# A transformer layer on one core: the second feed-forward product split into rounded high and low parts

## The reference

```python
q, k, v = x @ w_q, x @ w_k, x @ w_v            # 16 heads of 64
p = softmax(causal_mask(q @ k.T / 8))          # per head, 1024 x 1024
x = layernorm(x + (p @ v) @ w_o)
h = x @ W_exp + b_exp                          # 128 -> 512
h = butterfly(h, up_weights)                   # 9 stages of 2x2 mixes over the 512 features
h = gelu(h + up_bias)                          # exact gelu
h = butterfly(h, down_weights)                 # 9 stages
y = h @ W_con + b_con                          # 512 -> 128
x = layernorm(x + y + down_bias)
```

## Time and profile before

| | |
|---|---|
| median of 3 runs | 1036.63 us (1035.93 to 1037.27) |
| profiled execution: span from the first to the last instruction | 1033.9 us, some 2.7 us under the median |
| instructions | 17745 |
| attention, up to the first up product of group 0 | 968.2 us |
| feed-forward part and end | 65.7 us |
| PE busy | 1007.6 us, 97% of the span |

### The profile page before, as it was taken

One profiled execution on the slowest core, in us unless ns is written; L12 is line 12 of the kernel. 1 busy time (PEld: TensorE's weight loads), 2 busy tenths in 40 slices (PEclk: granted clock), 3 DMA queues, 4 the chain that ended last, 5 costly groups with the idle time before them and its releaser, 6 DMA issues.

```text
span 1033.9 us, 17745 instructions
## 1 busy us (share of the span) xinstructions
PE 1007.6 (97%) x5816; PEld 697.8 (67%) x5816; DVE 772.2 (75%) x2093; ACT 612.4 (59%) x1245; POOL 760.4 (74%) x739
## 2 busy tenths in 40 slices
PE   6899999999999999999999999999999999999997
PEld 4566676676766676676666776667666766665697
DVE  8767777777777777877788787877778787875364
ACT  3556655666655656566655656666555656665543
POOL 7567887777768887777778887777778987777414
PEclk8799999999999999999999999999999999999999
DMA  6233222233222222232222222332223222320002
GB/s 190 62 85 81 51 65 54 60 83 84 63 63 62 66 68 55 63 83 63 77 69 62 63 53 55 81 83 63 76 50 80 62 57 53 83 64 22 22 11 73
DMA packets 48603, 68.72 MB, mean 66 GB/s; under 512 B 15191, under 2 KB 25083, under 8 KB 48510
## 3 DMA queue, kind: packets, MB, share of 16 engines
q1 hardware_dynamic: 48510, 67.57, 25.3%
HBM read 31.11 MB, written 2.36 MB: 32 GB/s over the span
## 4 chain that ended last, share of the span: by engine, by line
PE 88%; DMA 5%; DVE 3%; ACT 1%; issue 1%; POOL 1%; SPq 0%; ACTq 0%; POOLq 0%
PE O L722 25%; PE WORK L636 13%; PE SC L697 13%; PE SC L701 12%; PE WORK L649 6%; PE WORK L684 3%; PE WORK L612 3%; PE WORK L613 3%; PE WORK L614 3%; DMA R<-RROW 2%; PE WORK L777 2%; DMA RROW<-RCOL 1%; PE WORK L622 1%; PE WORK L624 1%; PE WORK L623 1%; DVE WORK L989 1%
## 5 line engine op out<-in xcount | busy, mean ns | idle before, releaser
L868 ACT ACTIVATE PR<-SC 128x512 f32<-128x512 f32 (+3 forms) x768 | 352.3, 490 | 263.7 <-PE SC L701 234.8
L517 POOL TENSOR_TENSOR SUM<-SUM,PR 128x1024 f32<-128x1024 f32 (+3 forms) x256 | 419.3, 1638 | 14.9 <-POOL SUM L526 0.5
L989 DVE CUSTOM_DVE_ANT_0 WORK<-WORK,CMASK 128x128 f32<-128x128 f32 (+3 forms) x512 | 239.3, 514 | 64.8 <-PE WORK L636 64.7
L697 PE MATMUL SC<-QH,KHL 128*128 128x512 f32 (+3 forms) x768 | 269.3, 356 | 3.1 <-ACT PR L868 3.1
L701 PE MATMUL SC<-QL,KH 128*128 128x512 f32 (+3 forms) x768 | 262.0, 347 | 2.8 <-DMA QL<-NROW 2.8
L502 POOL TENSOR_SCALAR_AFFINE_SELECT PR<-PR 128x256 f32<-128x256 f32 x256 | 106.0, 415 | 198.6 <-ACT PR L868 198.5
L636 PE MATMUL WORK<-KHL,QH 128*128 128x512 f32 (+3 forms) x768 | 226.2, 365 | 4.3 <-DMA KH<-KHL 3.3
L722 PE MATMUL O<-PR,VLO 128*64 128x512 f32 (+3 forms) x1024 | 199.9, 522 | 0.6 <-DVE OT L1073 0.2
L697 PEld LDWEIGHTS SC<-QH,KHL 128*128 128x128 f32 x768 | 145.5, 189 | 61.2 <-ACT PR L868 28.9
L636 PEld LDWEIGHTS WORK<-KHL,QH 128*128 128x128 f32 x768 | 136.7, 191 | 57.1 <-issue 34.5
L992 DVE TENSOR_REDUCE MP<-WORK 128x1 f32<-128x512 f32 x256 | 164.3, 684 | 4.7
(11 more groups left out here) (129 smaller groups left out, 1099.6 us busy)
## 6 DMA issues: line engine op xcount, KB each, us to landing
QH<-QH SPq DMA_DIRECT2D x128, 128.0 KB, 2.3
KH<-KHL SPq DMA_DIRECT2D x128, 128.0 KB, 2.3
R<-RROW SPq DMA_DIRECT2D x64, 256.0 KB, 3.9
SW<-in_L_ffn_up_weights_dram SPq DMA_DIRECT2D x9, 512.0 KB, 4.3
SW<-_L_ffn_down_weights_dram SPq DMA_DIRECT2D x9, 512.0 KB, 4.6
out_dram<-X SPq DMA_DIRECT2D x7, 256.0 KB, 2.3
X<-in_L_attn_x_BSE_dram SPq DMA_DIRECT2D x3, 512.0 KB, 4.2
X<-in_L_attn_x_BSE_dram SPq DMA_DIRECT2D x2, 256.0 KB, 3.0
```

The lines of the kernel that those rows point to most:

```text
L517: nc.gpsimd.tensor_tensor(total, total, prob(unit, s), ALU.add).then_inc(add_done, 1)
L697: nc.tensor.matmul(dst, KHL[:, par, h, kt * P:(kt + 1) * P], QH[:, par, h, q0:q0 + n], start=True, stop=False)
L868: nc.scalar.activation(prob(unit, s)[:, h, :], SC[use % NSC][:, 0:n], ACT.Exp, scale=K ** -0.5).then_inc(exp_done, 1)
L989: op = nc.vector.tensor_tensor_reduce(cols, cols, CMASK[:, CH - n:], 1.0, LOWEST, ALU.add, ALU.max, cell)
```

## The change

W2 is no longer copied to SBUF as fp32: ACT writes its high part to W2H and DVE its low part to W2L (in the space of XTH and XTL). The Gelu result of each group, 128 x 2048 values, is split the same way: ACT copies the high part (one instruction), and the low part is G - hi, by POOL alone for groups 0 to 2, and by DVE (first half of the columns) and POOL (second half) for groups 3 to 7. The parts lie in four pairs of slots in QH, QL, KHL and KH1, which the attention and the up products have finished reading (`SPLIT_PAIR`). The tables `SPLIT_AFTER` and `DVE_SPLIT_AFTER` say after which group's Gelus, and after which `residual` or `deviation`, a split stands in the list of its engine. `down(g)` then makes three fp32r products in place of one fp32 product: hi x W2H, hi x W2L, lo x W2H. It waits for the splits (`split_lo`, `split_lo_dve`); a Gelu waits for the split of the group whose place in G it takes, not for the down product.

```diff
--- before.py
+++ after.py
@@ -120,6 +120,11 @@
 FFN_PIECES = [(g * TPC, (g + 1) * TPC) for g in range(B * CHUNKS - 1)]
 FFN_PIECES += [(B * TILES - TPC, B * TILES - 2), (B * TILES - 2, B * TILES)]
 ACT_RESULTS = 3
+SPLIT_PAIR = [0, 1, 2, 0, 1, 2, 0, 3]
+POOL_SPLITS = 3
+SPLIT_ORDER = [0, 1, 2, 3, 4, 5, 7, 6]
+SPLIT_AFTER = {0: [0], 1: [1], 3: [2], 5: [3], 6: [4], 7: [5, 7, 6]}
+DVE_SPLIT_AFTER = {0: [3], 1: [4], 2: [5, 7], 3: [6]}
 X1_AT = {("x1", g): (UNITS - 1, g + 2 + 4 * (g > 2), 2) for g in range(EARLY_GROUPS)} | {("w2", 0): (UNITS - 1, 11, 2)}
 NORMALISE_AT = {t: ((t // TILES + 1) * PAIRS + 3 + t % TILES, 10) for t in range((B - 2) * TILES)}
 NORMALISE_AT |= {t: ((B - 1) * PAIRS + 3 + t % TILES // 2, 9 + t % 2) for t in range((B - 2) * TILES, (B - 1) * TILES)}
@@ -257,6 +262,11 @@
         up_b_row = w2t[0:1, :]
         x1_hi_slots = [T[:, 0, h, c * CH:(c + 1) * CH] for T in (QH, QL) for h in range(2) for c in range(CHUNKS)]
         x1_lo_slots = [T[:, 0, h, c * CH:(c + 1) * CH] for T in (KHL, KH1) for h in range(2) for c in range(CHUNKS)]
+        parity = lambda T, n: T[:, n, :, :].rearrange("p h s -> p (h s)")
+        split_pairs = [(parity(QH, 1), parity(QL, 1)), (parity(KHL, 1), parity(KH1, 1)),
+                       (parity(QH, 0), parity(KHL, 0)), (parity(QL, 0), parity(KH1, 0))]
+        W2H = XTH[:, 0:HID].rearrange("p (t d) -> p t d", t=HT)
+        W2L = XTL[:, 0:HID].rearrange("p (t d) -> p t d", t=HT)
         W1H = WST[:, :, :, :].rearrange("p a n c -> p (a n c)")
         W1L = WSV[:, :, :].rearrange("p a c -> p (a c)")
         wqkv_flat = WQKV[:, :, :].rearrange("p n c -> p (n c)")
@@ -298,6 +308,7 @@
         h1_added, stats_made = sem("h1_added"), sem("stats_made")
         x1_made, x1t_made, x1t_copied = sem("x1_made"), sem("x1t_made"), sem("x1t_copied")
         x1t_hi, w1_hi, w1_lo = sem("x1t_hi"), sem("w1_hi"), sem("w1_lo")
+        w2_hi, split_hi, split_lo, split_lo_dve = sem("w2_hi"), sem("split_hi"), sem("split_lo"), sem("split_lo_dve")
         hid_ready, gelu_done, y_ready, h2_made = sem("hid_ready"), sem("gelu_done"), sem("y_ready"), sem("h2_made")
         out_made, act_out_made, out_stored = sem("out_made"), sem("act_out_made"), sem("out_stored")
         shift_mult, shift_made = sem("shift_mult"), sem("shift_made")
@@ -350,6 +361,10 @@
             qc, kt = STEPS[s]
             n = CH - START[s] if n is None else n
             return PR[:, (unit * NS + s) % PRING, :, 0:n]
+
+        def hidden(g):
+
+            return G[g % (DOWN_LAG + 1)].rearrange("p t c -> p (t c)")
 
         block = ctx.enter_context(nc.Block())
 
@@ -563,8 +578,19 @@
                         compose(n)
                 add(u, NS - 1)
 
+            def split_low(k):
+
+                pool.wait_ge(split_hi, SPLIT_ORDER.index(k) + 1)
+                hi_part, lo_part = split_pairs[SPLIT_PAIR[k]]
+                cols = slice(0 if k < POOL_SPLITS else 2 * CH, HT * CH)
+                nc.gpsimd.tensor_tensor(lo_part[:, cols], hidden(k)[:, cols], hi_part[:, cols].bitcast(F32),
+                                        ALU.subtract).then_inc(split_lo, 1)
+
+            split_low(0)
+            split_low(1)
             pool.wait_ge(stats_made, B * TILES)
             deviation((B - 1) * TILES, B * TILES)
+            split_low(2)
             for n, (first, end) in enumerate(FFN_PIECES):
                 pool.wait_ge(x1_made, min(end, B * TILES))
                 pool.wait_ge(stats_made, B * TILES + end)
@@ -576,6 +602,8 @@
                     pool.wait_ge(shift_mult, n - ACT_RESULTS + 1)
                     nc.gpsimd.tensor_scalar(SHIFT[:, first:end], SHIFT[:, first:end], -1.0, None,
                                             ALU.mult).then_inc(shift_made, 1)
+                for k in DVE_SPLIT_AFTER.get(n, []):
+                    split_low(k)
 
 
         @block.tensor
@@ -766,16 +794,22 @@
                                      stop=True).then_inc(hid_ready, 1)
 
             def down(g):
-                pe.wait_ge(gelu_done, (g + 1) * HT)
+                pe.wait_ge(split_lo, SPLIT_ORDER.index(g) + 1)
+                if g >= POOL_SPLITS:
+                    pe.wait_ge(split_lo_dve, SPLIT_ORDER.index(g) + 1 - POOL_SPLITS)
                 if g < 2:
                     evacuated(LAST_OUT + g)
                     evacuated(NUMBER[UNITS - 1, ("w2", 0)])
                 else:
                     pe.wait_ge(h2_made, g - 1)
+                g_hi, g_lo = split_pairs[SPLIT_PAIR[g]]
                 for i in range(TPC):
+                    y = y_bank(g * TPC + i)[:, i * P:(i + 1) * P]
                     for t_ in range(HT):
-                        t = nc.tensor.matmul(y_bank(g * TPC + i)[:, i * P:(i + 1) * P], G[g % (DOWN_LAG + 1)][:, t_, i * P:(i + 1) * P],
-                                             W2[:, t_, :], start=t_ == 0, stop=t_ == HT - 1)
+                        cols = slice(t_ * CH + i * P, t_ * CH + (i + 1) * P)
+                        nc.tensor.matmul(y, g_hi[:, cols], W2H[:, t_, :], start=t_ == 0, stop=False)
+                        nc.tensor.matmul(y, g_hi[:, cols], W2L[:, t_, :], start=False, stop=False)
+                        t = nc.tensor.matmul(y, g_lo[:, cols], W2H[:, t_, :], start=False, stop=t_ == HT - 1)
                     if any(end == g * TPC + i + 1 for _, end in FFN_PIECES):
                         t.then_inc(y_ready, 1)
 
@@ -826,9 +860,12 @@
             def evacuate(u, f, at):
 
                 w, free = WORK[at % NWORK], work_free[at % NWORK]
-                if f[0] in ("max", "out", "w2", "wo", "con", "bias"):
+                if f[0] in ("max", "out", "wo", "con", "bias"):
                     return
                 act.wait_ge(work_ready, at + 1)
+                if f[0] == "w2":
+                    hi(W2H, w[:, :].rearrange("p (t d) -> p t d", t=HT)).then_inc(w2_hi, 1)
+                    return
                 if f[0] == "x1":
                     hi(x1_hi_slots[f[1]], w[:, :]).then_inc(x1t_hi, 1)
                     return
@@ -901,13 +938,20 @@
                 for t_ in range(HT):
                     act.wait_ge(hid_ready, g * HT + t_ + 1)
                     if t_ == 0 and g > DOWN_LAG:
-                        act.wait_ge(y_ready, g - DOWN_LAG)
+                        act.wait_ge(split_lo, g - DOWN_LAG)
+                        if g - DOWN_LAG > POOL_SPLITS:
+                            act.wait_ge(split_lo_dve, g - DOWN_LAG - POOL_SPLITS)
                     nc.scalar.activation(G[g % (DOWN_LAG + 1)][:, t_, :], hid_banks[t_], ACT.Gelu,
                                          bias=BIAS1[:, t_:t_ + 1]).then_inc(gelu_done, 1)
                 n = g - (EARLY_GROUPS - 2)
                 if 0 <= n < B * CHUNKS - EARLY_GROUPS:
                     act.wait_ge(x1t_made, n + 1)
                     hi(x1_hi_slots[EARLY_GROUPS + n], O[(EARLY_GROUPS + n) % 2][:, :]).then_inc(x1t_hi, 1)
+                for k in SPLIT_AFTER.get(g, []):
+                    if k in (3, 4, 5, 6):
+                        act.wait_ge(y_ready, k - 3 + 1)
+                    act.wait_ge(gelu_done, (k + 1) * HT)
+                    hi(split_pairs[SPLIT_PAIR[k]][0], hidden(k)).then_inc(split_hi, 1)
             for n in range(ACT_RESULTS, len(FFN_PIECES)):
                 act.wait_ge(shift_made, n - ACT_RESULTS + 1)
                 for t in range(*FFN_PIECES[n]):
@@ -1042,8 +1086,8 @@
                     nc.vector.tensor_copy(BIAS1[:, :], w[:, 0:HT]).then_inc(free, 1)
                     dve.wait_ge(bc_made, 1)
                 elif f[0] == "w2":
-                    dve.wait_ge(work_ready, at + 1)
-                    nc.vector.tensor_copy(w2t, w[:, :]).then_inc(free, 1)
+                    dve.wait_ge(w2_hi, 1)
+                    lo(W2L, w[:, :].rearrange("p (t d) -> p t d", t=HT), W2H).then_inc(free, 1)
 
             def add_bc(g):
 
@@ -1143,6 +1187,10 @@
                     result(n - 1)
                 if n + EARLY_GROUPS < B * CHUNKS:
                     copy_x1t(n + EARLY_GROUPS)
+                for k in DVE_SPLIT_AFTER.get(n, []):
+                    dve.wait_ge(split_hi, SPLIT_ORDER.index(k) + 1)
+                    hi_part, lo_part = split_pairs[SPLIT_PAIR[k]]
+                    lo(lo_part[:, 0:2 * CH], hidden(k)[:, 0:2 * CH], hi_part[:, 0:2 * CH]).then_inc(split_lo_dve, 1)
 
 
 # ---- launch: one core; inputs and outputs as the reference has them ----
```

## The result

The changed kernel takes 1058.87 us (median of 4 runs, 1057.99 to 1059.16) against 1036.42 us for the kernel before (4 runs, 1035.93 to 1037.27): a ratio of 1.0215, 95% interval 1.0203 to 1.0227, or 22.5 us slower. The forecast was 1054.2, with a range of 1049 to 1062; the measured time is 4.7 us above the forecast. The profiled execution spans 1057.3 us, 23.4 more than the one of before.

What follows compares the result with a forecast made beforehand. PE was taken to bound the feed-forward part; 14.8 + 2.5 + 1.4 - 1.1 = +17.6 us on a span of 1033.9 gave 1051.5, plus 2.7 around the span 1054.2 us, range 1049 to 1062.

Steps and rivals of the forecast that it cites:

- part 1: Down products on PE: 48 fp32r products a group at 0.113 us each, 5.42 us a group, +14.8 us for eight.
- (b): Rival for the down products: loads overlap better, 0.085 us a product, eight groups +4.1 us, time 1043.5; chance 0.07.
- (c): Rival for the down products: 0.06 us is the true pace, eight groups save 5.4 us, time 1034.0; chance 0.03.
- part 2: Early phase: ACT's high-part copies of 1.9 us delay the output projection from 982.41 to about 984.9, +2.5 us.
- part 3: Low parts on POOL and DVE: POOL's split 2 delays DVE's normalisations and so group 6's transposes, +1.4 us (0 to 2).
- Split 3: Ahead of up 7: DVE's half goes first and is done when PE reaches up 7, no cost, no slack.
- rival (a): POOL holds the ports more: first at split 3 (+2.0, 1056.2), or fp32r writes cost double (1063.7); chance 0.14.
- should leave the clock alone: Early phase: PE's new gaps, under 2 us each, leave the granted clock at 1.00, no cost.
- Rival (d): Clock falls in the early-phase gaps: up 4 and down 0 at 1.2 GHz add some 3 us (1057); chance 0.03.
- Tail and W2: POOL's pieces no longer stack at the end, -1.1 us; W2's split goes into ACT's wait, 0, at most 0.6.

Runs made afterwards that it cites:

- products_alone: Changed kernel without the splits: Gelu writes rounded values itself and the third product takes them too, all 48 products a group kept; 1051.31 us (1.0139).
- experiment 4: Two runs on products_alone: each down product with 64 instead of 128 moving columns, 1074.65 us, or with 64 instead of 128 stationary columns, 1031.90 us.
- copies_late: both_orders with ACT's copies 0, 1, 2 a group or more later and POOL's split 1 behind the last deviation and the normalisations; 1051.13 us (1.0133).
- split3_late: Changed kernel with DVE's half of split 3 behind the residual of group 1 instead of ahead of it; 1055.51 us (1.0181).
- both_orders: Changed kernel with POOL's split 2 after DVE's eight normalisations and DVE's half of split 3 behind group 1's residual; 1052.46 us (1.0153).
- half_moving: products_alone with each down product streaming only the first 64 columns of its W2 tile, weight loads unchanged; 1074.65 us (1.0372).
- two_products_orders: both_orders without the third product (lo x W2H), so 32 products a group, all splits kept; 1049.03 us (1.0112).

## Why the prediction was right, and where it was short

The time lies in the stated range, and the largest terms came out to half a microsecond. But it lies outside the forecast's own narrower range, 1052 to 1057. Two terms that the sum had at nothing, up 7's wait and the clock, made the difference. The wide range held because it had been drawn to take in two rivals, of 2 and of 3 us, and something of both happened at once; that the sum of the two stayed inside is partly luck. One of the prediction's own signs of being wrong, a clock under 1.00 between 985 and 1045, did appear.

**The products** (part 1) were the main term: forecast 0.113 us and +14.8, measured 0.1115 and +14.3, and 14.1 us by themselves in products_alone, with the shorter tail in it. The choice between 0.06 and 0.12 went by the distance of the loads, and experiment 4 shows that this was the reason, not the gap between products: rivals (b) and (c) are out. The 81 ns of the Trainium skill's "TensorE: Matmul & The Clock Gate", section "Back-to-back issue gap", don't hold for fp32r at 128 columns (0.1115 here); the 107 ns of its "LDWEIGHTS (loading the stationary operand)" do.

**ACT's copies** (part 2): +2.5 forecast, +2.7 measured, with copies of 1.91 us. copies_late took it back: 15.9 over before fell to 14.0.

**Split 2** (part 3): +1.4 forecast, 1.5 measured. One detail was the other way round: no normalisation of DVE got in first. POOL began 0.06 us ahead of DVE, and DVE's first one waited out a POOL instruction of 4.55 us. So the lock that the skill's "SBUF — State Buffer", section "SBUF: two separate sides", describes holds for one so long, as the piece of 4.58 us in the chain shows.

**Split 3**: the step that failed is "I take DVE first, for its 0.03 us". POOL started at 1012.76, DVE stood ready at 1012.78, and up 7 waited 1.6 us, as rival (a) had it. The list had been worked out with "no slack"; with no slack a difference of 0.02 us between two engines decided over 2.4 us. No run has DVE first; by the prediction's 1.3 and 3.6 us from 1012.78 DVE would have been done at an estimated 1017.7, ahead of PE, whose last product of down 2 starts at 1018.04. split3_late, with DVE's half behind group 7's rows, shows that the order is what up 7 waited for.

**The clock** was the larger miss: "should leave the clock alone" was judged for the early gaps, and held there; the gaps after the down products, one of them forecast, were given no clock at all. Behind both it fell for about 3 us each, which cost 1.2 and 1.6 us. Rival (d) had nearly that price, but the wrong place. both_orders, without the two waits and at 1.00, is 6.4 us faster than the changed kernel, and 1.5 + 1.6 + 2.8 = 5.9 of these are in the account.

**Tail and W2**: -1.1 forecast, -1.0 measured; nothing of W2's cost is to be seen on PE. What stays open is the 1.6 us of the attention part in the profile (scatter, most likely, since it is there before the first edited instruction), and why the clock falls behind a gap of 0.9 us at 998 and not behind 1.2 us at 974 to 984.

## What to carry to other kernels

Count loads before columns: where an fp32r product here streamed no more columns than its load of 128, the load paced it, and splitting an fp32 product into three fp32r ones turned two loads into three; 48 loads for 32 were 14 us here, 32 for 32 nothing. An unbroken PE covers helpers' work, and a helper that makes PE wait costs its wait and, in the two cases here, about as much again in the clock. POOL's subtractions and DVE's normalisations or subtractions out of SBUF behaved as one queue here: write the order of such instructions out, rather than leave it to which is released first.

## What the runs showed of the hardware that I had not expected

- The clock can fall with PE never idle by its records (the ends of products are modelled): half_moving, loads of 128 with 64 moving columns, went from 1.00 to 0.62 over 994.7 to 997.5, and to 0.50 for the last 25 us, where its loads took 333 ns instead of 190.
- Once fallen it need not come back: in two_products_orders it stood at 0.50 over the last 16 us of unbroken down products, after one wait of 0.8 us; behind up products of 512 columns and under fp32 records it came back within some 3 us.
- Leaving out a third of the products made the kernel no faster (1058.35 and 1058.87 us).
